# A delta-rule layer's projections as three fp32r products, and its token mixer moved from matmuls to vector operations

## The reference, cut to what matters

```python
q = short_conv(x @ Wq, conv_q)            # 4 taps along the tokens, then silu
k = short_conv(x @ Wk, conv_k)
v = short_conv(x @ Wv, conv_v)
...                                       # rotary tables, 4 heads of 64
beta  = sigmoid(x @ Wb)
gamma = sigmoid(x @ Wgamma)
...                                       # per chunk of 32 tokens:
A = -(kb @ k.T) * strict_lower            # T = inverse of (I - A), by rows
u = T @ v ;  w = T @ kb
attn = q_i @ k_i.T * tril_inc
u_t  = u_i - w_i @ S
o_i  = q_i @ S + attn @ u_t
S    = g * S + k_i.T @ u_t
...
def fractal_mixer(x, conv_w):
    out = 2.0 * x
    for i in range(4):                    # shifts of 1, 2, 4 and 8 tokens
        out = out + shift(x, 2 ** i) * conv_w[i, :, 0] + x * conv_w[i, :, 1]
    return out
frac = rmsnorm(fractal_mixer(x, frac_conv_w), mixer_norm_w)
return rmsnorm(o) @ Wo + sigmoid(x @ frac_gate_w + b) * frac
```

## Time and profile before

| | |
|---|---|
| median of 3 runs | 2610.29 us |
| lowest, highest | 2605.36, 2612.67 us |
| profiled execution, its own time | 2605.69 us |
| its span | 2603.9 us |
| PE busy over the span | 93% |
| DVE, POOL, ACT busy | 65%, 51%, 47% |
| mean granted PE clock | 0.976 |

### The profile page before, as it was taken

One profiled execution on the slowest core, in us unless ns is written; L12 is line 12 of the kernel. 1 busy time (PEld: TensorE's weight loads), 2 busy tenths in 40 slices (PEclk: granted clock), 3 DMA queues, 4 the chain that ended last, 5 costly groups with the idle time before them and its releaser, 6 DMA issues. The chain is left out here.

```text
span 2603.9 us, 56605 instructions
## 1 busy us (share of the span) xinstructions
PE 2413.8 (93%) x20854; PEld 2007.2 (77%) x20854; DVE 1696.0 (65%) x4060; ACT 1216.3 (47%) x3095; POOL 1334.0 (51%) x1465
## 2 busy tenths in 40 slices
PE   4899999999999999878999999988899999999998
PEld 3788888888888888756777877756677778778776
DVE  4576777767677767576767767326756746747664
ACT  2656666666666666455444445114333333332332
POOL 3676776767676767256555555214522323322322
PEclk8999999999999999989999999988999999999999
DMA  4000100000000000012112111206112112212211
GB/s 141 7 10 9 45 17 11 9 10 10 10 10 9 9 5 5 15 31 45 42 47 49 36 53 43 55 31 187 33 52 68 62 42 74 66 42 62 64 39 58
DMA packets 156688, 105.05 MB, mean 40 GB/s; under 512 B 85168, under 2 KB 134832, under 8 KB 156416
## 3 DMA queue, kind: packets, MB, share of 16 engines
q1 hardware_dynamic: 131072, 62.83, 8.9%
q10 hardware_dynamic: 25344, 38.60, 4.8%
HBM read 80.51 MB, written 20.88 MB: 39 GB/s over the span
## 5 line engine op out<-in xcount | busy, mean ns | idle before, releaser
L920 POOL TENSOR_TENSOR a_bm<-a_bias,a_mask_add 128x512 f32<-128x512 f32 (+3 forms) x512 | 437.8, 871 | 191.0 <-DVE a_nm L674 186.0
L1529 POOL TENSOR_TENSOR m_hid_part<-m_hid,m_hid_part 128x512 fp32r<-128x512 f32 x176 | 239.5, 1361 | 564.1 <-ACT m_hid_part L1438 561.0
L830 ACT ACTIVATE a_S<-a_S,a_nm 128x512 f32<-128x512 f32 (+3 forms) x512 | 289.2, 565 | 346.4 <-DVE a_nm L674 343.6
L674 DVE CUSTOM_DVE_ANT_0 a_S<-a_S,a_bm,a_nsn 128x512 f32<-128x512 f32 (+3 forms) x512 | 275.4, 545 | 141.2 <-PE a_S L438 136.9
L461 PE MATMUL a_O<-a_v,a_PT 128*128 128x64 f32 x2560 | 342.4, 265 | 0.0
L461 PEld LDWEIGHTS a_O<-a_v,a_PT 128*128 128x128 f32 x2560 | 328.4, 193 | 0.0
L1450 ACT ACTIVATE m_hid<-m_G 128x512 f32<-128x512 f32 x176 | 105.4, 599 | 408.4 <-PE m_G L1384 371.3
L438 PE MATMUL a_S<-a_kT,a_qT 128*128 128x384 f32 (+3 forms) x1024 | 284.3, 359 | 3.5 <-DVE a_nm L674 3.0
L1401 PE MATMUL m_Y<-m_hid_part,m_down_high 128*128 128x512 f32 x704 | 257.3, 406 | 11.9 <-POOL m_hid_part L1529 11.1
L1611 DVE TENSOR_TENSOR m_hid<-m_hid,m_U 128x512 f32<-128x512 f32 x176 | 121.0, 687 | 223.6 <-PE m_U L1384 189.7
L1384 PE MATMUL m_G<-m_in,m_gate_high 128*128 128x512 f32 x704 | 251.5, 398 | 1.6 <-POOL m_up_low L1523 1.6
(11 more groups left out here) (314 smaller groups left out, 5240.2 us busy)
## 6 DMA issues: line engine op xcount, KB each, us to landing
m_spread<-s_w ACTq DMA_DIRECT2D x64, 256.0 KB, 3.3
m_spread<-s_w ACTq DMA_DIRECT2D x128, 128.0 KB, 2.9
a_x<-in_x SPq DMA_DIRECT2D x32, 128.0 KB, 2.1
s_hT<-a_hT SPq DMA_DIRECT2D x32, 128.0 KB, 2.1
d_x<-in_x SPq DMA_DIRECT2D x8, 512.0 KB, 4.8
d_h<-s_hT SPq DMA_DIRECT2D x8, 512.0 KB, 5.4
s_xg<-d_xg SPq DMA_DIRECT2D x8, 512.0 KB, 3.1
d_x<-s_xg SPq DMA_DIRECT2D x8, 512.0 KB, 4.5
```

The costliest lines, as they stand in the source:

```text
L674: dve.tensor_tensor_reduce(S[:, n % S_SLOTS, 0:w], SB[n % 2][:, 0:w], bm[:, n % BM_SLOTS, 0:w], -1.0, nsn[:, tile % 2, h:h + 1], ALU.add, ...
L830: act.activation(S[:, n % S_SLOTS, 0:w], S[:, n % S_SLOTS, 0:w], ACT.Exp, scale=-1.0, bias=nm[:, tile % 2, h:h + 1], accum_out=den[:, tile ...
L920: pool.tensor_tensor(bm[:, n % BM_SLOTS, 0:w], bias[:, h, L - w:L], mask_add[b % 2][:, 0:w], ALU.add).then_inc(s["bm_ready"], 1)
L1529: pool.tensor_tensor(hid_part[1][:, q % H_SLOTS], hid[:, q % G_SLOTS], hid_part[0][:, q % H_SLOTS].bitcast(F32), ALU.subtract).then_inc(hi ...
```

## The change

The inputs of the projections are split: `w_high` and `h_part[0]` are roundings to fp32r, `w_low` and `h_part[1]` are what is left, and a projection is the sum of high*high, low*high and high*low (`TERMS`), six matmuls of 512 tokens. The weights are split once, in the attention phase (ACT after tile 12, DVE after tile 16; `w_low` takes the place of `wqkv`). The input is split per sequence by the new piece `hs`, on ACT (a cast of 128x1024) and on DVE (a subtraction of 128x1024); for the first sequence both stand at the head of the delta phase.

The mixer leaves the matmuls: ACT makes `mx` = input times its own weight (`tap` 0 and 1, 128x512 each), DVE adds the four shifted inputs in place (`mix` 0 and 1, four operations of 128x512 each), and PE turns 128 tokens with two transposes (`mixer`, now with lag F, one round later, as are `frac`, `fve`, `frs`, `xg`). `diag` is gone. `vk` is single instead of double, the square in `frac` is written over PSUM. A piece `warm` (one unread matmul) stands at five places of every round from 2 on; `fast` issues three matmuls for b = 6 instead of two.

```diff
@@ delta_inputs
+    w_high = ctx.enter_context(nc.sbuf_tensor("d_wqkv_high", [P, KD, 3 * D], F32R))
+    with nc.sbuf_tensor("d_wqkv", [P, KD, 3 * D], F32) as wqkv:
+        pass
+    w_low = ctx.enter_context(nc.sbuf_tensor("d_wqkv_low", [P, KD, 3 * D], F32R))
@@ attention_phase, DVE
+                        if t == 4 * TT:
+                            dve.wait_ge(delta["high_ready"], 1)
+                            dve.tensor_tensor(delta["w_low"][:], delta["wqkv"][:], delta["w_high"][:].bitcast(F32),
+                                              ALU.subtract).then_inc(delta["low_ready"], 1)
@@ attention_phase, ACT
+                        if t == 3 * TT:
+                            act.wait_ge(delta["in"], 16 * len(delta["loads"]))
+                            act.copy(delta["w_high"][:], delta["wqkv"][:]).then_inc(delta["high_ready"], 1)
@@ delta_phase, tables
+        TERMS = [(j, s, k) for j, s in ((0, 0), (1, 0), (0, 1)) for k in range(KD)]
...
-            ("S", 10, R), ("x1", 1, K),
-            ("S", 11, R), ("fve", 0, IN), ("attn", 1, F), ("low", 0, IN),
+            ("S", 10, R), ("x1", 1, K), ("hs", 0, NX), ("mix", 0, IN),
+            ("S", 11, R), ("fve", 0, F), ("attn", 1, F), ("low", 0, IN), ("mix", 1, IN),
...
@@ SP
-                            sp.wait_ge(mixer_psum, TT * bi)
+                            sp.wait_ge(mix_ready, KD * bi)
+                            sp.wait_ge(proj_psum, 6 * bi)
+                            sp.wait_ge(gates_psum, bi)
                         sp.dma_start(h[(bi + 1) % 2][:, :, PAD:], hT_dram[bi + 2]).then_inc(h_in[(bi + 1) % 2], 16)
@@ PE
                     if name == "proj":
-                        if i == 0 and b > 0:
-                            pe.wait_ge(h_in[b % 2], 16 * ((b + 1) // 2))
+                        if i == 0:
+                            pe.wait_ge(h_high, b + 1)
+                            pe.wait_ge(h_low, b + 1)
                         o = fill(name, i, b)
-                        for k in range(KD):
-                            last = pe.matmul(o[:, :], wqkv[:, k, i * P:(i + 1) * P], h[b % 2][:, k, PAD:],
-                                             start=k == 0, stop=k == KD - 1)
+                        for n, (j, s, k) in enumerate(TERMS):
+                            last = pe.matmul(o[:, :], wqkv[j][:, k, i * P:(i + 1) * P], h_part[s][:, k],
+                                             start=n == 0, stop=n == len(TERMS) - 1)
                         last.then_inc(proj_psum, 1)
+                    elif name == "warm":
+                        unread(fill(name, i, b), 1)
                     elif name == "fast":
-                        unread(fill(name, i, b), B - b)
+                        unread(fill(name, i, b), 1 if b == B - 1 else 3)
...
                     elif name == "mixer":
+                        pe.wait_ge(mix_ready, KD * (b + 1))
                         o = fill(name, i, b)
                         for k in range(KD):
-                            at = PAD + i * P
-                            for j in range(5):
-                                back = 0 if j == 4 else 2 ** j
-                                last = pe.matmul(o[:, k * P:(k + 1) * P],
-                                                 h[b % 2][:, k, at - back:at - back + P], diag[:, k, j],
-                                                 start=j == 0, stop=j == 4)
+                            last = pe.transpose(o[:, k * P:(k + 1) * P], mx[:, k, i * P:(i + 1) * P], ident[:])
@@ ACT
+                def input_high(b):
+                    if b == 0:
+                        act.wait_ge(delta["h0_in"], 16)
+                    else:
+                        act.wait_ge(h_in[b % 2], 16 * ((b + 1) // 2))
+                        act.wait_ge(proj_psum, 6 * b)
+                    act.copy(h_part[0][:], h[b % 2][:, :, PAD:]).then_inc(h_high, 1)
+
+                input_high(0)
...
+                    elif name == "tap":
...
+                            act.wait_ge(mixer_psum, TT * b)
+                        act.activation(mx[:, i], h[b % 2][:, i, PAD:], ACT.Copy, scale=own[:, i:i + 1]).then_inc(mix_tap, 1)
@@ DVE
+                def input_low(b):
+                    dve.wait_ge(h_high, b + 1)
+                    dve.tensor_tensor(h_part[1][:], h[b % 2][:, :, PAD:], h_part[0][:].bitcast(F32),
+                                      ALU.subtract).then_inc(h_low, 1)
+
+                input_low(0)
...
+                    elif name == "mix":
+                        dve.wait_ge(mix_tap, KD * b + i + 1)
+                        for j in range(4):
+                            at = PAD - 2 ** j
+                            ins = dve.scalar_tensor_tensor(out=mx[:, i], in0=h[b % 2][:, i, at:at + L],
+                                                           scalar=frac[:, i, j, 0:1], in1=mx[:, i],
+                                                           op0=ALU.mult, op1=ALU.add)
+                            if j < 3:
+                                link(ins)
+                        ins.then_inc(mix_ready, 1)
```

More of the change, by code:

```diff
@@ L1679, in delta_phase @@
         sb, bank, sem, sems = space(nc, ctx, "d")
-        wqkv, wsm, smb, conv, frac, cos, sin, rot, mixw, strict, causal, chunk_of, side, eye16, corner, wo, onw, x = (
-            delta[n] for n in ("wqkv", "wsm", "smb", "conv", "frac", "cos", "sin", "rot", "mixw", "strict", "causal",
+        wsm, smb, conv, frac, cos, sin, rot, mixw, strict, causal, chunk_of, side, eye16, corner, wo, onw, x = (
+            delta[n] for n in ("wsm", "smb", "conv", "frac", "cos", "sin", "rot", "mixw", "strict", "causal",
                                "chunk_of", "side", "eye16", "corner", "wo", "onw", "x"))
         own = sb("own", [P, KD])
-        diag = sb("diag", [P, KD, 5, P])
+        mx = sb("mx", [P, KD, L])
         cm = sb("cm", [P, TT, H2, DH // 2])
@@ L1688, in delta_phase @@
         half = sb("half", [P, TT * H2])
+        wqkv = [delta["w_high"], delta["w_low"]]
         h = [delta["h0"], sb("h1", [P, KD, PAD + L])]
+        h_part = [sb(f"h_part{j}", [P, KD, L], mybir.dt.float32r) for j in range(2)]
         xg = sb("xg", [P, TT, D])
@@ L1761, in delta_phase @@
         nb_ready = sem("nb_ready")
+        own_ready = sem("own_ready")
+        mix_tap = sem("mix_tap")
+        mix_ready = sem("mix_ready")
         mixer_psum = sem("mixer_psum")
@@ L1972, in _ @@
                 pe.wait_ge(*loaded)
+                pe.wait_ge(delta["low_ready"], 1)
                 pe.wait_ge(delta["h0_in"], 16)
@@ L2273, in _ @@
                 link(dve.tensor_reduce(own[:], frac[:, :, :, 1], AX.X, ALU.add))
-                link(dve.tensor_scalar(own[:], own[:], 2.0, None, ALU.add))
-                for k in range(KD):
-                    for i in range(5):
-                        w = own[:, k:k + 1] if i == 4 else frac[:, k, i, 0:1]
-                        dve.tensor_scalar(diag[:, k, i], ident[:], w, None, ALU.mult)
+                dve.tensor_scalar(own[:], own[:], 2.0, None, ALU.add).then_inc(own_ready, 1)
                 dve.wait_ge(rot_ready, 1)
@@ L2287, in _ @@
                 for name, i, b in pieces(DVE_ROUND):
-                    if name == "conv":
+                    if name == "hs":
+                        if b > 0:
+                            input_low(b)
+                    elif name == "conv":
                         w = conv[:, i // 2, i % 2]
```

99 lines of the change are left out of this document (54 added, 45 removed).

## The result

The changed kernel takes 2693.6 us (median of 4 runs, 2691.1 to 2694.5), the kernel before 2611.4 us in the same comparison: ratio 1.0318, 95% interval 1.0300 to 1.0336. The forecast was 2613 us, 2588 to 2632. The span of the profiled execution is 2689.3 us against 2603.9: 85.4 us more.

What follows compares the result with a forecast made beforehand. PE bounds rounds 3 to 7 now, but a DVE-POOL path would hold them at 69.5 us. Terms summed to +5.2 on 2605.7, giving 2610.9, or 2615.5 on the median's scale; 2613 us was taken, range 2588 to 2632.

Steps and rivals of the forecast that it cites:

- Attention phase: One more ACT pass and one more DVE pass of 128x1536, in queues with slack: +1 us (0 to 3.4).
- head: Start of the delta phase: PE waits for cast and subtraction, then has shorter projections: together -1 us (-2.5 to +2.2).
- rounds 0 and 1: Rounds without a scan, waiting on the path: the new chain behind `conv` 5 delays `low` 1, +6 and +6.2 us.
- Round 2: Round without `ors`, so POOL has no slack to give: +0.5 us.
- Rounds 3 to 7: Five steady rounds, each falling from 71.0 to 69.5 us: -7.5 us in all.
- All of them before `low` 1: DVE's eight additions and subtraction, 7.2 us a round, stand before `low` 1, where the 8.4 us of slack are.
- Of the path only POOL's wait of 1.46 us goes: Path around the round from `low` 1 through inversion and DVE-POOL hand-over to the next `low` 1: 71.0 - 1.5 = 69.5 us.
- the PE case: Rival: PE stays the bound, its 61.2 us plus some 3 of waits a round; rounds 3 to 7 -34, time 2587; chance 0.22.
- The clock: Two existing clock falls of 3.5 us each cost half with slack on PE, but there may be more: -4 us (-7 to +21).
- The rival in which it falls in every round: Clock falls from `M` 3 over `step` 2 to `Z`, 3.5 us each: 2627 to 2634; chance 0.28.
- The last rounds: Behind the last `Z`: 11 `fast` with one matmul more, eight `warm`, two mixers' transposes: +4 us.
- The additions: Eight on DVE at 0.74 us a round; with the subtraction, DVE's queue takes back what the mixer left on PE.

Runs made afterwards that it cites:

- e13_dense: Changed kernel with `x1` 0 early, `proj` 4 back, `warm` out of the ring, `z` 0's wait filled, `z` 2 before `Z` 0, plus 26 unread wide matmuls a round: 2621.7 us.
- e14_no_additions: Changed kernel with the eight 512-column additions left out, one 128-column addition standing for each four: 2691.5 us, ratio 1.0305.
- e7_both: Changed kernel with `x1` 0 ahead of `rotb` 2 in DVE's queue and `proj` 4 before `au` 0 again: 2649.1 us, ratio 1.0165.
- e1_filled_gaps: Changed kernel with 8, 5, 6 and 16 unread matmuls laid at `qp` 0, `z` 0, `z` 2 and `uw` 0: 2673.2 us, ratio 1.0258.
- e12_bank_wait_in_before: Kernel before with three unread pieces of one matmul each put behind `core` 0: 2640.9 us, ratio 1.0121.

## Why the prediction was wrong

**Attention phase, head, rounds 0 and 1 (+1, -1, +6, +6.2).** DVE's timeline of the changed kernel:

```profile
1145.03 2.32 DVE L2338 SCALAR_TENSOR_TENSOR d_y<-d_proj,d_conv,d_y 128x512 f32<-128x512 f32 x3
1149.59 1.23 DVE L2312 TENSOR_TENSOR d_h_part<-d_h,d_h_part 128x1024 fp32r<-128x1024 f32 x1 [2.24 <-ACT d_h_part L2204]
1150.73 3.11 DVE L2347 SCALAR_TENSOR_TENSOR d_mx<-d_h,d_frac,d_mx 128x512 f32<-128x512 f32 x4
1153.76 0.42 DVE L2418 TENSOR_TENSOR d_low<-d_R,d_nb 128x256 f32<-128x256 f32 x1
1154.09 3.10 DVE L2347 SCALAR_TENSOR_TENSOR d_mx<-d_h,d_frac,d_mx 128x512 f32<-128x512 f32 x4
1157.11 0.42 DVE L2418 TENSOR_TENSOR d_low<-d_R,d_nb 128x256 f32<-128x256 f32 x1
```

From the end of `conv` 5 (1147.35) to `low` 1 it is 9.8 us, as the sum had it; in round 1 (1208.64 to 1219.67) 11.0 against 11.1. But `conv` 5 of round 0 ended 2.2 us later than before, where the head and the attention phase together were put at nothing. The last transposes of the attention phase start at 1096.4 for 1093.0, so that phase gave +3.4 for +1 (1095.0 to 1098.6 in the other kernels with the split, 1093.0 to 1094.8 in those without), and the head -1.2 for -1. Round 2 gave -0.1 for +0.5.

**Rounds 3 to 7 (-7.5).** This step failed: +59.5. It was built on two sentences. "All of them before `low` 1" and "`low` 1 would start at 1413.6" were right (15.7 us after `qk` 3 for 14.8; 14.7 in `e13_dense`). "Of the path only POOL's wait of 1.46 us goes" was not. The path's middle was taken as fixed because PE had no part in it before; but DVE's queue in it holds eight `S`, each waiting for a `step` of PE. The forecast counted what the change put on PE and never walked PE's own order for new waits. Two stood there to be found: `au` 0 without the projection before it (named in passing, at the PE case, and not priced), and the bank of `uw` 0. That one needs only the list of pieces and the number five. Undoing them brought the mean round from 84.3 to 77.1, the rest of the ring with the filled wait before `z` 0 to 74.4, and the density to 70.5, 1 us above the forecast.

**The clock (-4).** The rival in which it falls in every round was the right mechanism, and named the place of the first two of the four low stretches of a round; the others lie behind `Z`. Its price was wrong: 3.5 us a fall, from a kernel in which one short fall met a dense PE. Here the clock of 0.80 means its lower level for 40% of the round, 34 us, and the slowed `step` 2 and `step` 8 make DVE and POOL wait. That these waits come back to PE and lower the clock again is argued; no run takes it apart. The rival's 2627 to 2634 was 60 us short or more.

**The last rounds (+4)** gave 12.3, at a clock of 0.82 for 0.90. **The additions** were priced at all of PE's gain; in the changed kernel they cost nothing measurable (`e14_no_additions`), in the dense one they are in the 14.7 us. **The PE case** had PE's sum right: 69.4 busy in `e13_dense`, less 5.7 for its 26 matmuls and 0.9 for four more in `z`, is 62.8 for the 61.2 of the sum. The path it doubted was there.

What stays open: why `e7_both` alternates, what the wide matmuls of `e13_dense` would do in the changed kernel with its waits left in, and what `e13_dense` would be without the additions; none was tried.

## What to carry to other kernels

Work taken off an engine that bounds a kernel uncovers waits in its own queue; before pricing a gain, walk that queue in its new order for each wait that the removed or moved piece had covered. Where pieces share banks in turn, a new or moved piece shifts the bank of every later one: list for each piece whose bank it inherits, and who frees it. A moved piece can also hold up an engine that only issues DMAs, if something in its program waits for that piece. And wide matmuls that look like waste to be moved may be what holds PE's clock; replace them by as much dense work, or price every matmul of the stretch at the lower level.

## What the runs showed of the hardware

The three waits of PE shown above, 1.2 to 3.9 us, went with stretches at a granted clock of 0.50 of 7 to 14 us; where unread matmuls of 512 columns filled the first of them, the clock stayed at 1.00. A wait of 1.8 us before `z` 3 in `e1_filled_gaps` passed without a fall, so a wait of this length does not always bring one. The Trainium skill (TensorE: Matmul & The Clock Gate, Why this matters for your kernels) warns of idle gaps between bursts of matmuls, but only of gaps longer than the first two waits here. The trace agrees for the wait of 3.9 us; those of 1.8 and 1.2 us are shorter than what that advice speaks of, and yet stood at two falls, in stretches of thin matmuls. And idle time was not needed: in the kernel before and in `e12_bank_wait_in_before` (1457) the clock fell while PE was busy all the time, with 32x64 and 128x64 matmuls for the most part, and with 26 wide ones a round it stayed at 1.00 in three of five rounds of `e13_dense`. That unread work makes a round shorter, 70.5 us for 74.4, I had not expected in that size.
